# Narrowing the DMA waits ahead of the split of three weight sums in a two-layer gated recurrence

## The reference, cut to what matters

```python
xz = jnp.einsum('btd,de->bte', seq, W_z)
xr = jnp.einsum('btd,de->bte', seq, W_r)
xh = jnp.einsum('btd,de->bte', seq, W)

def step(h, xs):
    xzt, xrt, xht = xs
    z = jax.nn.sigmoid(xzt + h @ U_z + vz)
    r = jax.nn.sigmoid(xrt + h @ U_r + vr)
    hh = jnp.tanh(xht + r * h @ U + vh)
    h_new = (1.0 - z) * h + z * hh
    return (h_new, h_new)
```

## Time and profile before

| | |
|---|---|
| median of 3 runs | 1542.58 us (1542.54 to 1543.11) |
| the profiled execution | 1542.05 us, of which the span from first to last instruction is 1540.3 us |
| TensorE busy | 1518.5 us, 99% of the span, 24290 matmuls |
| VectorE busy | 1320.4 us, 86% |
| ScalarE busy | 1043.5 us, 68% |
| GpSimd busy | 301.8 us, 20% |
| mean granted TensorE clock | 0.995 |
| DMA, mean over the span | 76 GB/s |
| chain that ended last | TensorE 94%, VectorE 2%, DMA 1%, ScalarE 1%, issue 1% |

### The profile page before, as it was taken

One profiled execution on the slowest core, in us unless ns is written; L12 is line 12 of the kernel. 1 busy time (PEld: TensorE's weight loads), 2 busy tenths in 40 slices (PEclk: granted clock), 3 DMA queues, 4 the chain that ended last, 5 costly groups with the idle time before them and its releaser, 6 DMA issues.

```text
span 1540.3 us, 57130 instructions
## 1 busy us (share of the span) xinstructions
PE 1518.5 (99%) x24290; PEld 1177.0 (76%) x24290; DVE 1320.4 (86%) x2921; ACT 1043.5 (68%) x2422; POOL 301.8 (20%) x329
## 2 busy tenths in 40 slices
PE   9999999999999999889999999999999999999998
PEld 6875544444444467666799999999999999999998
DVE  7999889998999889787888888888888888887787
ACT  6989799999999823334566666666666666656333
POOL 1100111111110012213222222222222222222222
PEclk9999999999999999999999999999999999999999
DMA  5056355565639866535333333333333333320000
GB/s 195 28 157 215 78 154 163 120 164 134 184 87 146 118 108 53 70 50 72 45 21 47 25 44 48 21 48 48 21 48 44 24 48 20 47 41 3 32 31 31
DMA packets 544159, 116.80 MB, mean 76 GB/s; under 512 B 520096, under 2 KB 526496, under 8 KB 535200
## 3 DMA queue, kind: packets, MB, share of 16 engines
q1 hardware_dynamic: 536896, 82.73, 31.0%
q0 software_dynamic: 7008, 30.41, 10.5%
HBM read 66.47 MB, written 33.55 MB: 65 GB/s over the span
## 4 chain that ended last, share of the span: by engine, by line
PE 94%; DVE 2%; DMA 1%; ACT 1%; issue 1%; SPq 0%; POOL 0%; DVEq 0%; ACTq 0%; POOLq 0%
PE ps L1373 33%; PE ps L1475 21%; PE ps L1438 20%; PE ps L1487 11%; PE ps L1459 7%; PE ps L1391 2%; PE ps L1340 1%; DVE ST L1218 1%; DMA raw<-in_x 0%; DMA AR<-Lb 0%; DMA AR<-Y 0%; DMA SWfrom<-Lb 0%; PE ps L1404 0%; DVE RL L1253 0%; DVE XP L1185 0%
## 5 line engine op out<-in xcount | busy, mean ns | idle before, releaser
L1373 PE MATMUL ps<-XH,WH 128*128 128x512 f16 x1872 | 404.7, 379 | 0.0
L1373 PEld LDWEIGHTS ps<-XH,WH 128*128 128x128 f16 x1872 | 183.1, 98 | 220.2 <-issue 0.3
L1475 PE MATMUL ps<-HL,U 128*128 128x64 f16 x7888 | 271.6, 193 | 1.7 <-DVE HL L1297 1.7
L1475 PEld LDWEIGHTS ps<-HL,U 128*128 128x128 f16 x7888 | 255.4, 98 | 9.5 <-issue 2.7
L1586 POOL TENSOR_TENSOR ST<-ST 128x256 f32<-128x256 f32 x127 | 106.3, 837 | 478.9 <-ACT ST L818 478.9
L796 ACT ACTIVATE ST<-ST 128x128 f32<-128x128 f32 x254 | 71.9, 309 | 170.5 <-DVE ST L1218 170.2
L1487 PE MATMUL ps<-HL,U 128*128 128x64 f16 x4064 | 166.5, 195 | 0.0
L1218 DVE SCALAR_TENSOR_TENSOR ST<-ps,dn,AR 128x128 f32<-128x128 f32 (+1 forms) x320 | 109.2, 372 | 44.6 <-PE ps L1487 42.7
L1475 PE MATMUL ps<-RL,U 128*128 128x64 f16 x3824 | 133.0, 193 | 11.2 <-DVE RL L1253 8.4
L1218 DVE SCALAR_TENSOR_TENSOR ST<-ps,dn,XP 128x128 f32<-128x128 f32 x315 | 107.4, 372 | 42.3 <-PE ps L1487 39.9
L1475 PEld LDWEIGHTS ps<-RL,U 128*128 128x128 f16 x3824 | 128.6, 98 | 19.4 <-issue 13.1
(11 more groups left out here) (196 smaller groups left out, 2947.8 us busy)
## 6 DMA issues: line engine op xcount, KB each, us to landing
x_scratch<-AR SPq DMA_DIRECT2D x16, 1024.0 KB, 5.3
AR<-in_x POOLq DMA_DIRECT2D x15, 1024.0 KB, 8.1
AR<-HB POOLq DMA_DIRECT2D x11, 1024.0 KB, 7.0
raw<-x_scratch SPq DMA_DIRECT2D x88, 128.0 KB, 4.4
out_y<-raw SPq DMA_DIRECT2D x11, 1024.0 KB, 4.2
raw<-in_x SPq DMA_DIRECT2D x10, 1024.0 KB, 7.6
ST<-in_x SPq DMA_DIRECT2D x5, 1024.0 KB, 7.6
out_y<-AR SPq DMA_DIRECT2D x4, 1024.0 KB, 4.6
```

Source lines behind the costliest of these rows:

```text
L1373: op = pe.matmul(ps[b][:, :], v[:, g, wp, k, e * P:(e + 1) * P], y[:, xp, k, :], start=n == 0, stop=n == 11)
L1475: pe.matmul(ps[b][:, col:col + B], U[:, g, uh, k, e * P:(e + 1) * P], S[:, k, 0], start=opens, stop=False, skip_group_check=True)
```

## The change

Rows 0 and 1 of a weight's sums are now split once the DMAs into quarters (0,1) and (0,0) have landed (m = 2 and 3), rows 2 and 3 once those into (1,1) and (1,0) have (m = 1 and 4). Nothing else is different; no instruction is added, removed or put in another place.

```diff
             def sw_hi(i, k):
-                for m in range(1, 5):
+                for m in ((2, 3) if k < 2 else (1, 4)):
                     act.wait_ge(d_sums[i, m], 16)
                 act.activation(SW[i][:, 0, k], by_k(sw_from[i])[:, k], ACT.Copy, scale=up[:, scale(i)]).then_inc(s_swhi, 1)
```

## The result

The changed kernel takes 1526.99 us (median of 4 runs, 1525.47 to 1527.41) against 1542.83 us (4 runs, 1542.54 to 1543.11): a ratio of 0.9896 with a 95% interval of 0.9878 to 0.9913, 15.8 us less. 1526.7 had been predicted. The profiled execution took 1527.41 us with a span of 1525.6.

A forecast was written before the change was run, and what follows sets the result against it. TensorE, busy 1518.5 of 1540.3 us, was taken as the bound, with a DMA holding ACT and so TensorE. Stalls of 6.36, 4.67 and 4.83 us sum to 15.9, from 1542.6 to 1526.7 us; range 1525.4 to 1530.8.

The forecast's parts named there:

- Rows 0 and 1 cost nothing afterwards: ACT's split right after hn: its own work delays step 9's sigmoid by at most 0.2 us, put at nothing.
- Rows 2 and 3 find the DMA landed: Rows still wanting m = 4: split at 640.4, DMA landed at 629.43, 11 us left, so no cost.
- First stall: Step 9 becomes like its neighbour: 14.38 - 8.02 = 6.36 us won, nothing taken off for DVE.
- Third stall: Step 19: 12.92 - 8.09 = 4.83 us won, nothing given back since DVE has slack.
- 0.3 us: Step 15, at 8.43 in the trace, was already 0.3 us above the others; subtracted from DVE's give-back.
- Second stall: Step 13: 13.48 - 8.01 = 5.47 us, less 0.8 given back by DVE's lateness in steps 13 to 15: 4.7 us.
- The bound of 2 us: Upper bound on the second stall's give-back: DVE's lateness in each of steps 14 to 16 paid in full.
- The clock's share: Matmuls at a lower clock after each stall: the rest of the 15.9 us beyond 11.2 idle, less DVE's 0.8.
- DVE as the bound (1): Steps 9 to 17: DVE sets the pace, 2.4 to 4.8 us given back, 1528.3 to 1530.7 us; chance 0.13.
- That only the idle time comes back (2): Lower clock stays without the stalls; only the idle 11.2 us are won, 1531.4 us; chance 0.04.
- that the wait moves to row 2 (3): ACT stalls two steps later, needing a 15 us DMA; 1542.6 us or part of the way; chance 0.03.
- that the clock swings (4): Steps 13 to 16: small waits put TensorE at 1.2 GHz; with three such steps 1550.7 us; chance 0.03.

The follow-up runs named there:

- first_row_only: The kernel before, with only row k = 0 of each gate leaving out the waits on m = 1 and m = 4: 1527.4 us.
- gate1_waits_all: The changed kernel, with gate 1 waiting for all four adding DMAs again: 1531.82 us.
- gate1_low_twice: The changed kernel, with DVE making each of gate 1's four low halves twice: 1531.53 us.
- before_again: The kernel before, unchanged, run once more: 1542.84 us (10 runs).
- early_last_dma: The kernel before with all its waits, but POOL issues the fourth adding DMA ahead of its addition of hn in the same step: 1534.7 us.
- gate2_waits_all: The changed kernel, with gate 2 waiting for all four adding DMAs again: 1531.42 us.
- gate2_low_twice: The changed kernel, with DVE making each of gate 2's low halves twice: 1528.91 us.

## Why the prediction was right

*What bounds the kernel, and that the DMA holds ACT and ACT holds TensorE:* right. Restoring a gate's waits restores its stall, and two kernels that keep most or all waits but meet them late lose all three stalls.

*Rows 0 and 1 cost nothing afterwards:* right. The sigmoids of step 9 started at 625.90, 0.39 us after DVE's addition began (625.51). So they came as soon as its first half was there, ACT's own work added nothing, and step 9 took 8.01 us.

*Rows 2 and 3 find the DMA landed:* right, and with room: in `first_row_only` even row 1 does.

*First stall, 6.36 us:* 14.21 - 8.01 = 6.20. *Third stall, 4.83 us:* 12.76 - 8.08 = 4.68. Both terms were too large by 0.15 us, by the way I had measured. The windows of the earlier trace rows began where TensorE's timeline has the step's first product, but ended where the chain of waits has it, and the chain begins a piece only where the one before it ends, 0.16 us later. Step 15's 8.43 has the same fault; it is 8.27, with 8.15 for the next. With it goes the "0.3 us" by which I took step 15 to wait.

*Second stall, 5.47 less 0.8:* the 5.47 is right, DVE's give-back was 1.09: step 13 is 8.27 in the place of 8.01, step 14 is 8.84 in the place of 8.01, step 15 is 8.27 as before. I had 0.2, 0.7 and 0.15 less 0.3. The mechanism was right and the give-back a third larger than forecast; `gate1_waits_all` and `gate1_low_twice` show that it is DVE, and the row that I had named, line 1261 in step 14, is the one that TensorE waits for. The bound of 2 us held. Step 15 is no fixed term: with the stall in it took 8.27, 8.07 (`before_again`) and 8.00 (`gate1_waits_all`), so the give-back is 1.1 to 1.4 us by the execution that one compares with.

*The sum:* 15.9 us were forecast; the steps in the trace give 15.27, the medians 15.8. The terms were 0.6 us too large together, and that the medians' difference comes within 0.1 us of them is luck: whole runs of the changed kernel differ by 2 us among themselves.

*The clock's share, which I put in full:* right in sum, but not all of it is the clock's. In the trace of before the three stalled steps have 1.78, 1.54 and 1.81 us beyond idle time and normal length. Stalled steps in which the clock stayed at 1.00 have such a rest too: 0.68 and 0.49 us in `early_last_dma`, 0.49 in `gate2_waits_all`, with short waits of TensorE in it for line 1261 (0.35) or for the new state (0.15, 0.16). By these, an estimate for the clock alone is 0.9 to 1.3 us a stall. "A stall is paid twice" leaves that third part out; the forecast was not hurt by it, since it took whole step lengths.

*The rivals.* DVE as the bound (1) was there to a third of its price. That only the idle time comes back (2), that the wait moves to row 2 (3) and that the clock swings (4) didn't happen. Waits of up to 0.9 us ahead of four steps in a row, and single ones of 1.4 and 2.1 us, left the clock at 1.00. The Trainium skill, "TensorE: Matmul & The Clock Gate", section "A second HAM failure mode: psum-queue depth-cycling", describes a kernel whose TensorE idles briefly between groups of matmuls so often that its rate swings. No run here shows that; four such waits in a row are the most that was tried.

## What to carry to other kernels

A wait costs what is queued behind it in the engine's own order. The instruction that waited here was of no urgency at all, but the sigmoid of the next step stood behind it, so ask of every wait in an in-order engine whether it names only the data that the instruction reads, or whether the instruction could stand one step later. When stalls go, look which engine was resting in them, and judge its spare time by the place of the work in the step, between what it waits for and who waits for it, and not by its busy share.

## What the runs showed of the hardware

The price of a stall on TensorE isn't fixed. With idle times equal within 0.2 us, the same step took from 14.21 to 15.57 us, and another from 11.59 to 12.93, as the clock was low for longer, for less long or not at all afterwards. Some 3 us of idling in step 19 (2.9 and 3.0) lowered it in two executions and left it alone in one (3.0). The idle time of the shortest stall that lowered it was 2.9 us, of the longest that didn't 3.0. Ten runs of the kernel with three stalls lie between 1540.35 and 1545.16, eight of that with none between 1525.47 and 1528.6. The stalls may be a part of the wider spread, but the stretches ahead of step 9 and from step 20 on differ too, by 3.6 and 2.8 us over the traces.

An adding DMA of 256 KB took 4.6 to 4.8 us from issue to landing in one place of the step and 5.1 to 7.7 in another some 3 us earlier, so most of the earlier issue was lost in two of three cases.

Of a DVE and a POOL instruction that overlap, the one that began second took longer. A low half of 0.74 us took 1.11 when it began 0.17 us after POOL's multiplication (671.84 and 671.67, above). In `gate2_low_twice` the order is the other way round, and there POOL's instruction is the one that is longer, 1.17 us in the place of 0.73, with DVE at its usual 0.75:

```profile
717.20 0.75 DVE L1069 SCALAR_TENSOR_TENSOR AR<-AR,up 128x512 f16<-128x512 f32 x1
```

```profile
717.36 1.17 POOL L1591 TENSOR_TENSOR ST<-ST 128x256 f32<-128x256 f32 x1 [3.25 <-ACT ST L819]
```

The Trainium skill, "SBUF — State Buffer", section "Who interferes with whom", says that a VectorE instruction with two inputs from SBUF contends with a GpSimd instruction that reads SBUF, and that issue order decides who waits. These rows agree. The second instruction wasn't held for the whole overlap: it took 0.37 us longer at an overlap of 0.56 us, and 0.44 at one of 0.59.
